# Four graph layers in one pipelined kernel: weight preparations as once-only operations in the engines' lists, and new lists, lags and banks

## The chip, the cores and the metric

One NeuronCore of a Trainium2 chip runs the kernel. The metric is the device time of one execution in microseconds (us). The engines work beside each other, each through its own list of instructions in order, and meet in semaphores: TensorE (PE) multiplies matrices and transposes, and writes to eight banks of PSUM; VectorE (DVE), ScalarE (ACT) and GpSimd (POOL) work elementwise; SyncE (SP) and ACT issue transfers (DMAs).

## The reference

```python
h = relu(layernorm(x)); x = x + L0(h)   # x: (128, 128, 256) f32, adj: (128, 128)
h = relu(layernorm(x)); x = x + L1(h)
h = relu(layernorm(x)); x = x + L2(h)
h = relu(layernorm(x)); x = x + L3(h)
# L0: deg * (h @ Wi.T + b) + adj @ (h @ Wj.T)
# L1: Wh = h @ W; logits e_src[i] + e_dst[j], leaky relu, masked by adj, softmax, attn @ Wh
# L2: the same with 128 columns: concat(alpha @ h', h')
# L3: q, k, v = h @ W.T + b, 8 heads of 32, masked softmax(q k / sqrt(32)) v, then @ Wo.T + bo
```

128 graphs of 128 nodes are independent of each other; all share the adjacency and the weights.

## The kernel before

The 128 graphs are worked off as 64 pairs. A pair has some 100 operations (three to 32 instructions each), and the kernel is a software pipeline over steps t: every engine has one list of operations, `step(t)`, and an operation with lag LAG[name] works in step t on pair t - LAG[name], where there is such a pair (`due`). The order of the entries of LAG (lines 29 to 40) is the order of the calls in the lists: SP's first, then PE's, ACT's, DVE's and POOL's. Steps 7 to 62 are full (PE has lags from -1 to 7); those before are the opening, those after the end. A step's number is a label on each engine: an operation waits for the semaphores of what it needs (`passed`), for the readers of the buffer that it overwrites (`read_before`, buffers of two pairs mostly, one for the exps and probabilities of layer 3), and on PE for the last user of its PSUM bank (`bank_free`, table BANKS in lines 43 to 73: bank, operation that begins the use, operations that free it).

The operations by name, with a number for the layer: `stats`, `mv`, `veps` (DVE) and `rstd`, `y` (POOL) are the layernorm; `h0t` to `h3t` (PE) transpose y; `h.t_hi` (ACT) and `h.t_lo` (DVE) apply relu and split the value into two fp32r parts, since products of that type are made as three matmuls (lines 839 to 841). Layer 0: `m0`, `m1` (PE, the two graphs), `mj_hi` (ACT), `mj_lo` and `t0` (DVE, t0 reads `r0` = x + deg * b of POOL), `s0` (PE, aggregation), `x1` (DVE, line 480). Layer 1: `wh0`, `wh1` by PE as `wh0_mm`, `wh1_mm` and copied by ACT; `dst1` (POOL) gathers the column e_dst; SP writes it to memory (`row_out1`, line 239) and reads it back spread over the partitions (`row_in1`, line 245); `z1` (ACT, line 712) is the leaky relu of the sums, `nmax1` (DVE), `exp1` (ACT), `e1t` (PE), `at1` (ACT), `x2_mm` (PE), `x2` (DVE). Layer 2 is the same with `hh`, `dst2`, `row_out2`, `row_in2`, `z2` and so on, up to `x3` and POOL's `x3_tail`. Layer 3: `qt`, `kt`, `v`, `scores` (PE, 32 matmuls), `nmax3_j` (DVE), `exp3_j` (ACT), `p3_j` (POOL), `pt_j` (PE), `p3t_j` (ACT) for four groups of heads j, `ot` (PE), `ot_hi`, `ot_lo`, `x4_mm` (PE), `x4` (DVE, line 568), `store` (SP). `r3` (POOL) is x3 + bias.

Preparations that happen once stand before the lists or inside one operation's first call: POOL makes deg_b ahead of the first r0 and splits four weights ahead of the first rstd2 (`split_w3`); PE transposes the adjacency before its list, into bank 4, and multiplies weights with the attention vectors ahead of the first s0 (`multiply_weights`), also in bank 4; DVE copies the adjacency and makes the low part of w0 ahead of the first h0t_lo, and splits w1 ahead of the first h1t_lo; ACT rounds w0 ahead of the first h0t_hi.

Of the kernel before, what the change touches and what calls it, by code (L numbers as in the profile page):

```python
# [45 lines left out]
    "h2t": (4, "h2t", ('ht2',)),
    "at2": (3, "e2t", ('at2',)),
    "h1t": (0, "h1t", ('h1t_lo',)),
    "ot": (5, "ot_mm", ('ot_lo',)),
# [1 line left out]
    "sc1": (4, "scores", ('nmax3_1',)),
    "sc2": (3, "scores", ('nmax3_2',)),
    "sc3": (1, "scores", ('nmax3_3',)),
    "hh": (6, "hh_mm", ('hh',)),
    "x3b": (5, "x3_mm", ('x3',)),
    "wh1": (0, "wh1_mm", ('wh1',)),
# [1008 lines left out]
```

## Time and profile before

| | |
|---|---|
| runs | 1285.4, 1282.49, 1284.64 us; median 1284.64 |
| profiled execution | 1286.28 us, span 1284.5 us, clock 0.99 |
| PE busy | 1231.8 us (96%) |
| DVE busy | 1123.6 us (87%) |
| ACT busy | 1049.0 us (82%) |
| POOL busy | 944.6 us (74%) |
| DMA | 55.92 MB, mean 44 GB/s |

Busy time is the time with at least one instruction under way. On PE matmuls overlap, so one that lasts 0.28 us can be followed by the next after 0.12 us: the distance of starts tells the cost, not the duration. The span leaves out what lies around the first and the last instruction. Line numbers are those of the kernel before.

### The profile page before, as it was taken

Reading aid. Unit: us, or ns where it says so; the run is one execution under the profiler, and the core shown is the slowest. Engines: PE = TensorE matmul, PEld = TensorE weight load, DVE = VectorE, ACT = ScalarE, POOL = GpSimd, SP = SyncE. Lnnn points to the kernel's source line nnn. Section 1 sums busy time; section 2 is a strip of 40 time slices with the busy share of each in tenths; the row PEclk is TensorE's granted clock in tenths of the full one; section 3 lists DMA queues with packets and bytes.
Section 4 is the critical chain, followed back from the end, with each engine's and each line's share of the span. In section 5 each row is a group of like instructions: output and inputs, shape, how many; then the busy total and the mean of one; then the engine's idle time right before and its main releaser. Section 6 shows DMA issues by size and latency. Waiting matters only on the chain. (4 is left out here: it accounts for less than half of the span.)

```text
span 1284.5 us, 42963 instructions
## 1 busy us (share of the span) xinstructions
PE 1231.8 (96%) x12177; PEld 1135.2 (88%) x12177; DVE 1123.6 (87%) x5713; ACT 1049.0 (82%) x3907; POOL 944.6 (74%) x1360
## 2 busy tenths in 40 slices
PE   4589999999999999999999999999999999999987
PEld 3478999999999999999999999999999999999886
DVE  3678999999999999999999999999999999998774
ACT  1357888888888888888888888888888888888886
POOL 3657787787778778777777877877787787786654
PEclk8999999999999999999999999999999999999999
DMA  3121212221221221122122122223212212221110
GB/s 117 26 38 30 39 37 45 48 41 40 52 47 35 48 47 37 44 49 44 37 51 48 35 47 47 41 42 51 48 34 48 48 37 46 47 37 29 34 35 34
DMA packets 75768, 55.92 MB, mean 44 GB/s; under 512 B 23568, under 2 KB 75536, under 8 KB 75536
## 3 DMA queue, kind: packets, MB, share of 16 engines
q1 hardware_dynamic: 73472, 51.87, 20.4%
...
q14 instruction: 130, 1.06, 0.5%
...
## 5 line engine op out<-in xcount | busy, mean ns | idle before, releaser
L743 ACT ACTIVATE exps<-masked,nmax 128x128 f32<-128x128 f32 x1024 | 397.5, 400 | 0.0
L306 POOL TENSOR_TENSOR rstd<-veps,power 128x2 f32<-128x2 f32 x256 | 177.9, 695 | 230.3 <-DVE veps L458 230.1
L314 POOL TENSOR_SCALAR y<-x,nm,rstd 128x256 f32<-128x256 f32 x512 | 279.0, 557 | 4.2 <-issue 1.6
L342 POOL TENSOR_TENSOR probs<-exps,rsum 128x512 f32<-128x512 f32 x256 | 263.8, 1041 | 14.2 <-DVE rsum L553 14.2
L545 DVE CUSTOM_DVE_ANT_0 masked<-bank,mask 128x128 f32<-128x128 f32 x1024 | 233.3, 282 | 0.8 <-PE bank L945 0.8
L743 ACT ACTIVATION_READ_ACCUMULATOR exps<-masked,nmax 128x1 f32 x1024 | 203.8, 199 | 0.0
L839 PE MATMUL bank<-w_hi,ht_hi 128*128 128x512 f32 (+1 forms) x512 | 186.5, 364 | 7.0 <-DVE ht_lo L487 7.0
L442 DVE BATCH_NORM_STATS2 stats<-x 128x6 f32<-128x256 f32 x512 | 183.6, 410 | 3.9 <-DMA x<-in_x 3.8
L487 DVE SCALAR_TENSOR_TENSOR ht_lo<-bank,ht_hi 128x512 fp32r<-128x512 f32 x192 | 132.5, 690 | 52.0 <-ACT ht_hi L681 50.0
L849 PE MATMUL bank<-ident,y 128*128 128x128 f32 x1024 | 155.4, 275 | 21.6 <-POOL y L314 20.1
L841 PE MATMUL bank<-w_hi,ht_lo 128*128 128x512 f32 (+1 forms) x512 | 175.5, 343 | 0.0
L840 PE MATMUL bank<-w_lo,ht_hi 128*128 128x512 f32 (+1 forms) x512 | 175.3, 342 | 0.0
L681 ACT ACTIVATE ht_hi<-bank 128x512 fp32r<-128x512 f32 x192 | 114.8, 598 | 60.6 <-PE bank L849 60.4
L953 PE MATMUL bank<-ident,probs 128*128 128x128 f32 x1024 | 154.0, 274 | 3.7 <-POOL probs L342 1.8
L751 ACT ACTIVATE probs3t<-bank 128x512 f32<-128x512 f32 x256 | 152.2, 596 | 2.6 <-PE bank L953 2.6
L849 PEld LDWEIGHTS bank<-ident,y 128*128 128x128 f32 x1024 | 121.7, 142 | 33.1 <-POOL y L314 23.1
L953 PEld LDWEIGHTS bank<-ident,probs 128*128 128x128 f32 x1024 | 121.9, 141 | 11.8 <-POOL probs L342 3.9
L839 PEld LDWEIGHTS bank<-w_hi,ht_hi 128*128 128x128 f32 x512 | 98.4, 192 | 15.1 <-DVE ht_lo L487 8.5
L699 ACT ACTIVATE ht<-bank 128x512 f32<-128x512 f32 x64 | 38.2, 597 | 89.2 <-PE bank L849 89.2
L841 PEld LDWEIGHTS bank<-w_hi,ht_lo 128*128 128x128 f32 x512 | 98.1, 192 | 12.0
L840 PEld LDWEIGHTS bank<-w_lo,ht_hi 128*128 128x128 f32 x512 | 98.7, 193 | 6.4
L721 ACT ACTIVATE ez<-z,nmax 128x128 f32<-128x128 f32 x256 | 100.2, 393 | 2.1 <-DVE nmax L497 1.6
...
## 6 DMA issues: line engine op xcount, KB each, us to landing
x<-in_x SPq DMA_DIRECT2D x64, 256.0 KB, 5.5
db<-rows SPq DMA_DIRECT2D x128, 128.0 KB, 3.7
out<-x SPq DMA_DIRECT2D x64, 256.0 KB, 6.2
rows<-dst SPq DMA_DIRECT2D x128, 1.0 KB, 4.1
...
w_sb<-in_w ACTq DMA_DIRECT2D x1, 256.0 KB, 4.0
probs<-in_w1t ACTq DMA_DIRECT2D x1, 256.0 KB, 4.4
exps<-in_wot SPq DMA_DIRECT2D x1, 256.0 KB, 7.9
```

The source lines that it names most:

```text
L306: pool.tensor_tensor(rstd[i][:, b], veps[i][:, b], power[:], ALU.pow).then_inc(S[f"rstd{i}"], 1)
L314: last = pool.tensor_scalar(y[i][:, b, g], src[:, bx, g], nm[i][:, s, g:g + 1], rstd[i][:, s, g:g + 1], ALU.add, ALU.mult)
L342: pool.tensor_tensor(probs3[:, p % BUFFERS["probs3"], j], exps3[:, p % BUFFERS["exps3"], j], rsum3[:, s, j].unsqueeze(2).to_broadcast([P, ...
L442: last = dve.bn_stats(stats[i][:, b, g], src[:, bx, g])
L545: last = dve.tensor_tensor_reduce(masked3[:, b, j, i], bank_of(f"sc{j}")[:, i * P:(i + 1) * P], mask[:], scale=-1.0, scalar=-MASKED, op0=A ...
L743: last = act.activation(exps3[:, b, j, i], masked3[:, p % BUFFERS["masked3"], j, i], ACT.Exp, bias=nmax3[:, s, j, i:i + 1], scale=-1.0, ac ...
L751: act.activation(probs3t[:, b, j].rearrange("p b n -> p (b n)"), bank_of(f"pt{j}")[:], ACT.Copy).then_inc(S[f"p3t_{j}"], 1)
L839: pe.matmul(out_ap, lhs[0], rhs[0], start=start, stop=False)
L840: pe.matmul(out_ap, lhs[0], rhs[1], start=False, stop=False)
L841: return pe.matmul(out_ap, lhs[1], rhs[0], start=False, stop=stop)
L849: last = pe.transpose(bank_of(f"h{i}t")[:, (c * G + g) * P:(c * G + g + 1) * P], y[i][:, b, g, c * P:(c + 1) * P], ident[:])
L953: last = pe.transpose(bank_of(f"pt{j}")[:, i * P:(i + 1) * P], probs3[:, p % BUFFERS["probs3"], j, i], ident[:])
```

## The change

All lags, lists and banks are new; the once-only work becomes operations of its own in the lists, each with a lag that is its only step (`t == LAG[name]`), a semaphore, and for PE's two an entry in BANKS (`prepa`, `prep`). The rounding of the four layer-3 weights moves from POOL to ACT (`w3_high`), the four subtractions stay on POOL as `w3_low0` to `w3_low3` (wk, wq, wv, wo). The users wait for the new semaphores. The transfer of the bias moves from SP's fourth place to ACT's first, and ACT's loads of w1 and w2 behind its first activation. The loads' lag goes from -5 to -3. PE's lags are the old ones. The logits' rows go by transfers in both kernels.

```diff
 LAG = {
+       "row_out2": 3, "row_out1": 1, "row_in2": 3, "row_in1": 1, "store": 7, "load": -3, "qt_mm": 5, "h2t": 3, "kt_mm": 5, "h1t": 1, "e2t": 4,
+       "hh_mm": 3, "ot_mm": 7, "scores": 5, "adj_spread": -1, "x3_mm": 4, "wh1_mm": 1, "wh0_mm": 1, "e1t": 2, "pt3": 6, "h0t": -1, "x2_mm": 2,
+       "v_mm": 5, "s0": 0, "pt0": 6, "pt2": 6, "products": 0, "pt1": 6, "h3t": 4, "x4_mm": 7, "m1": -1, "m0": -1, "exp3_2": 5, "v": 5, "p3t_0": 6,
+       "p3t_2": 6, "w3_high": 0, "h3t_hi": 4, "z2": 3, "p3t_1": 6, "exp3_3": 5, "mj_hi1": -1, "mj_hi0": -1, "exp2": 3, "ht2": 2, "exp3_0": 5,
+       "h1t_hi": 0, "at2": 3, "w0_high": -3, "z1": 1, "hh": 2, "ot_hi": 6, "exp3_1": 5, "exp1": 1, "wh1": 0, "wh0": 0, "at1": 1, "p3t_3": 5,
+       "h0t_hi": -2, "nmax3_2": 5, "x3": 4, "rsum1_any": 2, "rsum3_1": 6, "stats3": 4, "rsum1": 2, "mv3": 4, "veps3": 4, "nmax3_3": 5, "h0t_lo": -1,
+       "x2": 2, "stats2": 2, "rsum3_2": 5, "mv2": 2, "adj_rows": -1, "nmax3_0": 5, "veps2": 2, "x1": 0, "h3t_lo": 4, "mv0": -2, "stats1": 0, "mv1": 0,
+       "veps0": -2, "veps1": 0, "nmax2": 3, "w1_split": 0, "x4": 7, "t0_1": -1, "nmax3_1": 5, "mj_lo1": -1, "mj_lo0": -1, "rsum3_3": 5, "t0_0": -1,
+       "qt": 4, "w0_low": -2, "kt": 4, "rsum3_0": 5, "rsum2": 3, "h1t_lo": 0, "nmax1": 1, "stats0": -3, "ot_lo": 6, "r0": -1, "rstd2": 2, "y2": 2,
+       "rstd1": 0, "y1": 0, "r3": 5, "w3_low2": 3, "x3_tail": 3, "p3_3": 5, "w3_low1": 1, "deg_b_made": -3, "rstd0": -2, "dst2": 2, "y0": -2,
+       "p3_0": 5, "dst1": 0, "p3_1": 5, "rstd3": 3, "y3": 3, "p3_2": 4, "w3_low0": 0, "w3_low3": 1,
 }
 BANKS = {
+    "qt": (0, "qt_mm", ('qt',)),
+    "h2t": (1, "h2t", ('ht2',)),
     "kt": (2, "kt_mm", ('kt',)),
+    "h1t": (3, "h1t", ('h1t_lo',)),
+    "at2": (4, "e2t", ('at2',)),
+    "hh": (5, "hh_mm", ('hh',)),
+    "ot": (1, "ot_mm", ('ot_lo',)),
     "sc0": (2, "scores", ('nmax3_0',)),
+    "sc1": (6, "scores", ('nmax3_1',)),
+    "sc2": (0, "scores", ('nmax3_2',)),
+    "sc3": (4, "scores", ('nmax3_3',)),
+    "prepa": (0, "adj_spread", ('adj_rows',)),
+    "x3b": (3, "x3_mm", ('x3',)),
+    "wh1": (5, "wh1_mm", ('wh1',)),
+    "wh0": (1, "wh0_mm", ('wh0',)),
+    "at1": (0, "e1t", ('at1',)),
+    "pt3": (5, "pt3", ('p3t_3',)),
+    "h0t": (3, "h0t", ('h0t_lo',)),
+    "x2b": (1, "x2_mm", ('x2',)),
+    "v": (5, "v_mm", ('v',)),
+    "x1b": (0, "s0", ('x1',)),
     "pt0": (3, "pt0", ('p3t_0',)),
+    "pt2": (4, "pt2", ('p3t_2',)),
+    "prep": (2, "products", ('w1_split',)),
+    "pt1": (5, "pt1", ('p3t_1',)),
+    "h3t": (1, "h3t", ('h3t_lo',)),
+    "x4b": (3, "x4_mm", ('x4',)),
+    "m1": (4, "m1", ('mj_lo1', 't0_1')),
+    "m0": (5, "m0", ('mj_lo0', 't0_0')),
 ...
@@ SP
-            sp.dma_start(deg_b[:], bias0.partition_broadcast(P)).then_inc(b0_in, 16)
@@ POOL
-                pool.wait_ge(deg_b_made, 1)
-            def split_w3():
-                pool.wait_ge(wk_in, 32)
 ...
-                for w, (hi, lo) in ((wk_sb, wk_r), (wq_sb, wq_r), (wv_sb, wv_r), (wo_sb, wo_r)):
-                    pool.tensor_copy(hi[:], w).then_inc(w3_high, 1)
 ...
+            def low_w3(i):
+                w, (hi, lo) = ((wk_sb, wk_r), (wq_sb, wq_r), (wv_sb, wv_r), (wo_sb, wo_r))[i]
+                pool.wait_ge(S["w3_high"], i + 1)
+                pool.tensor_tensor(lo[:], w, hi[:].bitcast(F32), ALU.subtract).then_inc(S[f"w3_low{i}"], 1)
             def biased_x0(p):
                 pool.wait_ge(x_in[bx], (p // BUFFERS["x0"] + 1) * 16)
+                pool.wait_ge(S["deg_b_made"], 1)
@@ DVE: the low part of w0 leaves prepare_rows
+            def low_w0():
+                dve.wait_ge(S["w0_high"], 1)
+                dve.tensor_tensor(w0_r[1][:], w0_sb, w0_r[0][:].bitcast(F32), ALU.subtract).then_inc(S["w0_low"], 1)
@@ ACT
-            act.dma_start(w1_sb[:, :, 0:D], w1.rearrange("(c p) o -> p c o", p=P)).then_inc(w1_in, 16)
+            act.dma_start(deg_b[:], bias0.partition_broadcast(P)).then_inc(b0_in, 16)
 ...
             act.activation(warm[:], power[:], ACT.Exp)
+            act.dma_start(w1_sb[:, :, 0:D], w1.rearrange("(c p) o -> p c o", p=P)).then_inc(w1_in, 16)
+            act.dma_start(w2_sb[:, :, 0:F1], w2.rearrange("(c p) o -> p c o", p=P)).then_inc(w2_in, 16)
 ...
+            def round_w3():
+                act.wait_ge(wk_in, 32)
 ...
+                for w, (hi, lo) in ((wk_sb, wk_r), (wq_sb, wq_r), (wv_sb, wv_r), (wo_sb, wo_r)):
+                    act.activation(hi[:], w, ACT.Copy).then_inc(S["w3_high"], 1)
@@ PE
+            def spread_adjacency():
+                pe.wait_ge(adjacency, 1)
+                bank_free(pe, "prepa", 0)
+                pe.transpose(bank_of("prepa")[:, 0:P], adj_f[:], ident[:]).then_inc(S["adj_spread"], 1)
             def multiply_weights():
-                pe.wait_ge(adj_t, 1)
+                bank_free(pe, "prep", 0)
 ...
@@ PE, project_transposed and project_v
-                pe.wait_ge(w3_split, 4)
+                for i in range(4):
+                    pe.wait_ge(S[f"w3_low{i}"], 1)
```

## Rows read from the trace of the kernel before

**Rows 1.** The table of stretches: us, busy us and (count) per engine, PEclk, DMA share, GB/s.
```profile
0.00:28.20 28.20, 11.65 (x40) 9.15 (x41) 8.78 (x32) 4.50 (x7) 9.68 (x17) 0.93 0.44 133
28.20:137.60 109.40, 88.59 (x633) 76.35 (x633) 83.37 (x383) 60.56 (x208) 71.59 (x110) 0.92 0.18 30
137.60:1192.20 1054.60, 1054.60 (x10636) 980.38 (x10635) 970.61 (x4974) 911.57 (x3415) 813.76 (x1171) 1.00 0.22 43
1192.20:1284.50 92.30, 76.93 (x875) 69.28 (x873) 60.85 (x326) 72.35 (x279) 49.55 (x62) 0.98 0.16 36
```

**Rows 2.** The source view of line 480, 200 to 1180 us.
```profile
L480 DVE TENSOR_TENSOR x<-bank,t x52: 690/690/693, 212.9 to 1174.0; 128x512 f32<-128x512 f32 x52
```

**Rows 3.** Timeline of the opening: start us, us, engine, line, operation, [idle before <-releaser].
```profile
5.85 0.74 DVE L442 BATCH_NORM_STATS2 stats<-x 128x6 f32<-128x256 f32 x2
...
9.17 0.61 POOL L289 TENSOR_TENSOR deg_b<-deg_b,deg 128x256 f32<-128x256 f32 x1 [7.68 <-DMA deg_b<-in_b]
...
10.90 0.75 DVE L442 BATCH_NORM_STATS2 stats<-x 128x6 f32<-128x256 f32 x2 [3.76 <-DMA x<-in_x]
...
11.98 2.14 POOL L314 TENSOR_SCALAR y<-x,nm,rstd 128x256 f32<-128x256 f32 x2 [0.19 <-POOL rstd L306]
...
14.17 1.12 PE L849 MATMUL bank<-ident,y 128*128 128x128 f32 x4 [8.43 <-POOL y L314]
...
25.26 2.06 PE L834 MATMUL bank<-exps,bv_sb 128*128 128x256 f32 x4
...
28.21 0.69 DVE L480 TENSOR_TENSOR x<-bank,t 128x512 f32<-128x512 f32 x1 [3.19 <-PE bank L867]
```

**Rows 4.** Timeline of POOL, 48 to 62 us.
```profile
49.61 0.61 POOL L298 CAST wk_hi<-exps 128x512 fp32r<-128x512 f32 x1
...
55.55 1.26 POOL L301 TENSOR_TENSOR wo_lo<-exps,wo_hi 128x512 fp32r<-128x512 f32 x1
```

**Rows 5.** Timeline of SP's queue, 63 to 92 us.
```profile
63.89 0.32 SPq L239 DMA_DIRECT2D rows<-dst  x1
...
68.66 0.32 SPq L245 DMA_DIRECT2D db<-rows  x1
...
69.08 0.59 SPq L239 DMA_DIRECT2D rows<-dst  x1
```

**Rows 6.** Timeline of ACT near the end.
```profile
1218.84 0.67 ACT L712 ACTIVATE bank<-db,wh 128x128 f32<-128x128 f32 x2 [2.49 <-DMA db<-rows]
```

**Rows 7.** Timeline of PE in one full step.
```profile
429.61 1.08 PE L965 MATMUL bank<-probs3t,v 128*32 128x128 f32 x32
...
431.72 1.16 PE L886 MATMUL bank<-w_sb,ht 128*128 128x130 f32 x8
...
432.72 0.61 PE L910 MATMUL bank<-hh,at 128*128 128x128 f32 x4
...
434.60 0.38 PE L902 MATMUL bank<-ident,ez 128*128 128x128 f32 x2
...
434.82 0.60 PE L953 MATMUL bank<-ident,probs 128*128 128x128 f32 x4
```

**Rows 8.** Timeline of ACT in the same step.
```profile
430.90 0.60 ACT L757 ACTIVATE ot_hi<-bank 128x512 fp32r<-128x512 f32 x1
...
431.38 0.41 ACT L743 ACTIVATE exps<-masked,nmax 128x128 f32<-128x128 f32 x1
...
432.92 0.39 ACT L705 ACTIVATE hh<-bank 128x260 f32<-128x260 f32 x1
...
434.80 0.39 ACT L693 ACTIVATE wh<-bank 128x258 f32<-128x258 f32 x1 [0.33 <-PE bank L841]
```

**Rows 9.** DMA issues, KB each, us to landing: 12 to 40 us, then 300 to 1100 us.
```profile
x<-in_x SPq DMA_DIRECT2D x3, 256.0 KB, 2.6
...
x<-in_x SPq DMA_DIRECT2D x43, 256.0 KB, 5.6
out<-x SPq DMA_DIRECT2D x43, 256.0 KB, 6.3
```

More of the change, by code:

```diff
@@ L29 @@
 LAG = {
[10 rows of a table removed]
[11 rows of a table added]
 }
 BANKS = {
-    "qt": (6, "qt_mm", ('qt',)),
+    "qt": (0, "qt_mm", ('qt',)),
+    "h2t": (1, "h2t", ('ht2',)),
     "kt": (2, "kt_mm", ('kt',)),
[L46 to L49, printed above, removed]
+    "h1t": (3, "h1t", ('h1t_lo',)),
+    "at2": (4, "e2t", ('at2',)),
+    "hh": (5, "hh_mm", ('hh',)),
+    "ot": (1, "ot_mm", ('ot_lo',)),
     "sc0": (2, "scores", ('nmax3_0',)),
[L51 to L56, printed above, removed]
-    "wh0": (3, "wh0_mm", ('wh0',)),
-    "at1": (6, "e1t", ('at1',)),
-    "pt3": (0, "pt3", ('p3t_3',)),
-    "h0t": (5, "h0t", ('h0t_lo',)),
-    "pt0": (3, "pt0", ('p3t_0',)),
-    "x2b": (6, "x2_mm", ('x2',)),
-    "pt2": (0, "pt2", ('p3t_2',)),
-    "x1b": (1, "s0", ('x1',)),
-    "v": (3, "v_mm", ('v',)),
-    "m0": (2, "m0", ('mj_lo0', 't0_0')),
-    "h3t": (0, "h3t", ('h3t_lo',)),
-    "pt1": (6, "pt1", ('p3t_1',)),
-    "m1": (5, "m1", ('mj_lo1', 't0_1')),
-    "x4b": (1, "x4_mm", ('x4',)),
+    "sc1": (6, "scores", ('nmax3_1',)),
[11 more added lines that the diff above has]
+    "x1b": (0, "s0", ('x1',)),
+    "pt0": (3, "pt0", ('p3t_0',)),
+    "pt2": (4, "pt2", ('p3t_2',)),
[5 more added lines that the diff above has]
+    "m0": (5, "m0", ('mj_lo0', 't0_0')),
     "zz2": (7, "z2", ('nmax2',)),
@@ L171, in gnn_kernel @@
         bank = [ctx.enter_context(nc.psum_tensor(f"bank{i}", [P, 512], F32)) for i in range(8)]
-        preparation = bank[4]
         def bank_of(task):
@@ L180, in gnn_kernel @@
         w0_in, w1_in, w2_in, wk_in, wq_in, wv_in, wo_in = [sem(f"{name}_in") for name in ("w0", "w1", "w2", "wk", "wq", "wv", "wo")]
[L181 to L183 removed]
+        constants, adjacency, w1_whole, w1_high, c3_made = [sem(name) for name in ("constants", "adjacency", "w1_whole", "w1_high", "c3_made")]
         x_in = [sem(f"x_in{i}") for i in range(BUFFERS["x0"])]
         x_out = [sem(f"x_out{i}") for i in range(BUFFERS["x4"])]
[L188 removed]
+        S = {name: sem(name) for name in LAG if name not in ("row_out2", "row_out1", "row_in2", "row_in1", "store", "load")}
         for name in ("nm0", "nm1", "nm2", "nm3",):
@@ L214, in bank_free @@
                 q = step - LAG[begun_by]
-                if other == number and 0 <= q < NP:
+                if other == number and 0 <= q < (1 if TASKS[i] in ("prepa", "prep") else NP):
                     for name in freed_by:
@@ L351, in step @@
             def step(t):
+                if due(t, "r0"):
+                    biased_x0(t - LAG["r0"])
+                if due(t, "rstd2"):
+                    inverse_deviation(2, t - LAG["rstd2"])
+                if due(t, "y2"):
+                    normalise(2, x2, t - LAG["y2"])
+                if due(t, "rstd1"):
+                    inverse_deviation(1, t - LAG["rstd1"])
+                if due(t, "y1"):
+                    normalise(1, x1, t - LAG["y1"])
+                if due(t, "r3"):
+                    biased_x3(t - LAG["r3"])
+                if t == LAG["w3_low2"]:
+                    low_w3(2)
+                if due(t, "x3_tail"):
+                    x3_tail(t - LAG["x3_tail"])
+                if due(t, "p3_3"):
+                    normalise_p3(3, t - LAG["p3_3"])
+                if t == LAG["w3_low1"]:
+                    low_w3(1)
+                if t == LAG["deg_b_made"]:
+                    prepare_deg_b()
+                if due(t, "rstd0"):
+                    inverse_deviation(0, t - LAG["rstd0"])
+                if due(t, "dst2"):
+                    gather_dst(2, hh, "hh", "hh", F1 + 1, t - LAG["dst2"])
+                if due(t, "y0"):
+                    normalise(0, x0, t - LAG["y0"])
+                if due(t, "p3_0"):
+                    normalise_p3(0, t - LAG["p3_0"])
+                if due(t, "dst1"):
+                    gather_dst(1, wh, "wh", last_of("wh0", "wh1"), D + 1, t - LAG["dst1"])
                 if due(t, "p3_1"):
@@ L926, in project_v @@
                 passed(pe, "h3t_lo", p)
-                pe.wait_ge(w3_split, 4)
+                for i in range(4):
+                    pe.wait_ge(S[f"w3_low{i}"], 1)
                 bank_free(pe, "v", p)
```

284 lines of the change are left out of this document (127 added, 157 removed), and 10 rows, old and new, of the table LAG.

## The prediction

> **What bounds the kernel now.** I read the table of stretches first [rows 1]. Columns: length, busy time and count of each engine, granted clock, DMA share, GB/s. Between 137.6 and 1192.2 us TensorE (PE) is busy in all of 1054.60 us at clock 1.00; VectorE (DVE) has 970.61 (92%), ScalarE (ACT) 86%, GpSimd (POOL) 77%. In the stretch there are 52 starts of the sum after layer 1 (x1, L480) from 212.9 to 1174.0 [rows 2]: 961.1 / 51 = 18.84 us per pair. The reader should see that 64 x 18.84 = 1206 us is PE's own work and that 1284.5 - 1206 = 78.5 us is all that an order of work alone can give back: PE idles 16.6 + 20.8 us in the opening (stretches 1 and 2 of rows 1) and 15.4 us at the end; the rest is half-clock time (0.93, 0.92, 0.98) and pipe filling. A list that makes PE wait in every step, though, costs 56 times (steps 7 to 62 are full).
>
> The change alters no PE operation and no PE lag: the PE pipeline stays 8 steps deep, and 18.84 us is the floor per full step. So the sum has an opening, an end, and a possible slip per full step.
>
> **A. Until the first x1 (28.21 us before).** POOL sat idle 7.68 us until the bias row had landed, made deg_b at 9.17, then r0, then rstd, and y0 only at 11.98, which took 2.14; the first transposes are at 14.17, on an engine idle for 8.43 us; the last four of the ten products of weights run at 25.26 for 2.06 us, ahead of the aggregation, and x1 starts at 28.21 [rows 3]. Now the bias is the first transfer of the ACT queue, r0 stands behind y0, and the products behind the aggregation. Statistics start at 5.85 for 0.74, some 0.5 more for mean and shift: 7.1; rstd 0.7: 7.9; y0 2.14: 10.0; transposes 1.12 and the ACT copy 0.6: 11.8. DVE holds the second tile's statistics before that (10.90 to 11.65, waiting for its landing), so it is free. ht_lo 0.7: 12.5 instead of 16.65. From there x1 took 11.56 us; 3.3 of it were the ten products and their weights (the timeline has them from 23.4 to 26.7, those of 25.26 last), so x1 starts at 12.5 + 8.3 = 20.8. Taken: -7.5. Ends: -4 (only the y0 part) and -10 (products and clock both kind). The products, 3.3 us or less, now delay m1 and m0 of pair 1, beside which x1, its statistics, rstd and y1 (some 3.5 us) and the split of w1 (2 us) run anyway: nothing, at worst +3, inside the ends.
>
> **B. Splitting the layer-3 weights.** Eight POOL operations from 49.61 to 56.81, 0.61 and 1.26 each, stood ahead of rstd and y [rows 4]: 7.2 us on the path, PE idle for 6 us behind them. Now ACT rounds them (4 x 0.6 = 2.4 us, step 0, where ACT next waits for m1; it has 48.8 of 109.4 us free in stretch 2 of rows 1) and POOL's four subtractions of 1.26 lie singly in steps 0, 1, 1 and 3, POOL being free for 38 of 109 us there. Each stands just after dst1 or y1, with at least 2 us until the next statistics. Taken: -6. Ends -3 (half come back) and -7.2.
>
> **C. Order of the row transfers, and y1 apart from y2.** SP issued layer 2's row at 63.89, and only after its landing the spread at 68.66 and layer 1's row at 69.08 [rows 5], though dst1 was ready at 66.3: 2.8 us, in the next step 2.3. The new SP list issues both rows before either spread. DVE and POOL now finish stats2, rstd2, y2 ahead of x1, stats1, y1, so y1 no longer queues behind y2: about 1 us per step in steps 2 to 4. PE work (15 us and more) bounds steps 5 and 6. Taken: -3. Ends 0 and -5.
>
> **D. The end.** In step 65 ACT idles 2.49 us before layer 1's logits, for a spread whose row was issued behind a store [rows 6]; PE then waits 2.0 and 1.1 us. The new list has the store after the spreads. The last chain (four exps of 1.54 us, POOL's probs, transposes, attention, projection) is the same. Taken: -3.5, ends 0 and -6.
>
> **E. A slip per full step.** In the new banks table pt3 takes bank 5, last used by wh1, so pt3 waits for ACT's copy of wh1. PE time from ot's start to pt3's: ot and scores 2.11 (429.61 to 431.72), x3 and the two wh 1.88 (432.72 to 434.60), e1t 0.22: 4.21; the 1.00 of hh now lies before ot [rows 7]. ACT's list in that time: ot_hi, exp3_1, exp1, wh1, for hh is now ahead of ot_hi. ot takes 1.08, ot_hi to the next 0.48, four exps 1.54, two more 0.77, the copy 0.39 [rows 7, 8], a semaphore 0.05: 4.31. ACT is not behind before ot_hi (ht2, exp3_0, h1t_hi, at2, z1, hh end 0.4 us before ot does). The loop ot - ACT - wh1 - pt3 - rest of the list - ot is therefore 0.10 too long, and a matmul that follows a wait is followed 0.05 later than in a stream: +0.15 per step, 56 steps, +8.4. Ends: 0 (ACT a tenth faster than its rows) and 0.3 (x2, which needs at1 1.1 us after e1t with 0.25 to spare, slips too), +17.
>
> A rule of the Trainium skill bears on that price: TensorE: Matmul & The Clock Gate (specifications table) says that the queue reorders in part and pulls weight loads ahead of matmuls in flight. If the waiting transposes' loads went ahead the slip would be nearer 0.05 per step, +3; the stalled matmuls of this trace show load and matmul starting together (both at 14.17), so I do not use it.
>
> The other reuses that I followed through the new lists have over 0.3 us: x4b after pt0 in bank 3 0.4, at1 to x2 0.25, wh0 after ot 0.8, e1t after sc2 0.7, h0t after x3b 0.9.
>
> **Sum** against the profiled run: 1286.28 us around a span of 1284.5. -7.5 - 6 - 3 - 3.5 + 8.4 = -11.6: 1274.7. The median of the runs shown, 1284.64, is 1.6 under the profiled run, so 1273.0.
>
> **Rivals.**
> 1. No slip. Speaks for it: a tenth of a us is within what overlapping ACT operations hide. Against: both sums come from rows of full steps. 1273.0 - 8.4 = 1264.6.
> 2. The load lands too late (slower). Lag -5 becomes -3, the lag of the statistics that read it, and the load is queued behind the store, which waits for x4. Loop in DVE: x4 - store issued 0.45 - load issued and landed L - stats0 - ot_lo - nmax3_2 - ... - x4. DVE is busy 17.3 us per step (970.61 / 1054.60 x 18.84); the operations outside this loop (t0, nmax3_1, mj_lo, qt, kt, h1t_lo, nmax1 and the small ones) make 5.2 of it, and small ones waiting for the one before add about 1: 13.1. The period is 13.5 + L, so it binds from L = 5.3. Loads landed in 2.6 us alone, in 5.6 in full steps, when they follow a row transfer and others come behind, stores in 6.3 [rows 9]. Ends for L: 2.6 and 6.3 or more. I take 4: the rows have landed by then, only the store is ahead. With L = 6.1 it is +0.8 x 56 = +45 and in place of E: 1273.0 - 8.4 + 45 = 1310. It decides from L = 5.3 + 20 / 56 = 5.7: above, the kernel is slower than before. The DMA chapter of the Trainium skill (DMA: Bandwidth & Descriptors, Queues, rings and completion order) speaks for this one: a completion increment is a strongly ordered write that lands only after all earlier writes of its DMA engine, so a load cannot report before the store has been written. By that rule L is at least the store's own landing less the 0.5 us between the issues, 5.8 if stores stay as they are in full steps; the trace has no load behind a store, so it neither shows nor excludes it.
> 3. The opening gains are given back: PE's half clock falls elsewhere, and products and subtractions delay steps 1 to 3. Half of A to C lost, 8.3: 1281.3. For it: three of the four half-clock spells lie where PE had waited; against: each edit takes away a wait seen in the trace.
> 4. The change does not do what it says: the opening steps are bound by the row transfers (rows, spread, logits, max, exps, e1t: 9.4 us from dst1) so that only the wait of B goes and E stays: 1286.3 - 6 + 8.4 - 1.6 = 1287, near the old time.
>
> **Chances.** Forecast 0.46 (1262 to 1281 for itself), no slip 0.22, late load 0.16, opening given back 0.12, row transfers 0.04. A measurement of this kernel can tell about 0.2%, 2.6 us, from no change. Faster by more: 0.45 + 0.22 + 0.02 + 0.07 = 0.76 (from the first four cases in this order); within: 0.01 + 0.01 + 0.03 + 0.02 = 0.07; slower: 0.13 + 0.02 + 0.02 = 0.17 (late load, opening, row transfers). The range takes in the first two whole and the third: 1262 to 1286.
>
> **What would show it.** x1 (L480's successor) first at about 20.8 us and for the eighth time at about 121 (A to C); no eight POOL operations in a row, deg_b near 5.5 us; SP issuing two rows back to back; no 2.49 us of ACT before the last logits. E: PE waits of about 0.1 us per full step for ACT's wh before transposes of probs, period 18.95 to 19.05. Rival 1: period 18.84. Rival 2: DVE stats waiting for DMA x in every full step, period above 19.2. I am wrong altogether if another engine pair waits more than 0.4 us in each full step, or if x1 comes first later than 24 us.

## The result

The changed kernel takes 1278.85 us (median of 8 runs, 1275.96 to 1279.74), the kernel before 1284.0 beside it (8 runs, 1282.49 to 1286.38): ratio 0.9959, 95% interval 0.9947 to 0.997. The forecast was 1273.0. The direction held and the time lies in the range, but the gain is 5.2 us where 11.6 were forecast.

The profiled execution took 1278.44 us around a span of 1276.6. Its table of stretches, cut at the same three events as [rows 1] (first x1, eighth x1, last x1, end), has the same columns: length, busy us and count for PE, PEld, DVE, ACT and POOL, granted clock, DMA share, GB/s.

```profile
0.00:22.44 22.44, 8.35 (x33) 6.33 (x33) 8.47 (x31) 5.87 (x10) 8.44 (x16) 1.00 0.60 167
22.44:123.89 101.45, 88.81 (x656) 77.14 (x656) 84.02 (x390) 61.91 (x211) 69.94 (x107) 0.95 0.20 32
123.89:1189.68 1065.79, 1065.79 (x10639) 986.88 (x10638) 1024.53 (x4977) 925.05 (x3416) 817.16 (x1173) 1.00 0.21 43
1189.68:1276.60 86.92, 75.19 (x858) 67.69 (x856) 60.03 (x321) 71.54 (x277) 48.76 (x61) 0.98 0.15 33
```

| stretch | before | after | change | forecast |
|---|---|---|---|---|
| to the first x1 (A) | 28.2 | 22.4 | -5.8 | -7.5 |
| to the eighth x1 (B, C) | 109.4 | 101.5 | -7.9 | -9.0 |
| 56 full steps (E) | 1054.6 | 1065.8 | +11.2 | +8.4 |
| from the last x1 (D) | 92.3 | 86.9 | -5.4 | -3.5 |
| span | 1284.5 | 1276.6 | -7.9 | -11.6 |

The kernel won 19.1 us outside the full steps and gave 11.2 back in them. Length less PE's busy time, from the two tables, tells where: between the first and the eighth x1 PE idles 12.6 us instead of 20.8 and is busy as long as before (88.8 us), so B and C are waits taken away. Up to the first x1 it idles 14.1 instead of 16.6 and is busy for 8.35 us instead of 11.65: most of the products now stand behind x1, and the granted clock is 1.00 instead of 0.93 (kernel 6).

**The opening**, as a timeline (start, us, engine, line, operation, idle before and its releaser), against [rows 3]:

```profile
7.31 0.23 DVE L395 CAST adj_f<-adj_i 128x128 f32<-128x128 int32 x1 [7.31 <-DMA adj_i<-in_adj]
...
8.24 0.74 DVE L441 BATCH_NORM_STATS2 stats<-x 128x6 f32<-128x256 f32 x2
...
10.45 2.13 POOL L304 TENSOR_SCALAR y<-x,nm,rstd 128x256 f32<-128x256 f32 x2 [0.19 <-POOL rstd L296]
...
22.44 0.68 DVE L479 TENSOR_TENSOR x<-bank,t 128x512 f32<-128x512 f32 x1
```

y0 comes at 10.45, earlier than the 11.98 of before but not at the 7.9 of the forecast: DVE starts its statistics at 8.24 instead of 5.85, for it idles until adj lands (deg_b, foreseen near 5.5, comes at 8.02). The bias, now first on ACT's queue, is the reason (kernel 5 below).

**Weights and rows.** The four subtractions of POOL lie singly; the first and the last of them, against [rows 4], then SP's queue, which now issues two rows together and then two spreads, against [rows 5]:

```profile
32.53 1.28 POOL L291 TENSOR_TENSOR wk_lo<-exps,wk_hi 128x512 fp32r<-128x512 f32 x1
...
63.57 1.27 POOL L291 TENSOR_TENSOR wv_lo<-exps,wv_hi 128x512 fp32r<-128x512 f32 x1
```

```profile
53.77 2.56 SPq L237 DMA_DIRECT2D rows<-dst  x2
57.81 1.20 SPq L243 DMA_DIRECT2D db<-rows  x2
```

**A full step.** The source view of the x1 sum (200 to 1180 us) gives (1171.1 - 200.3) / 51 = 19.035 us per pair, against 18.84 in [rows 2]. The timeline of PE and that of ACT show where, against [rows 7, 8]:

```profile
L479 DVE TENSOR_TENSOR x<-bank,t x52: 676/678/692, 200.3 to 1171.1; 128x512 f32<-128x512 f32 x52
```

```profile
460.17 0.43 PE L919 MATMUL bank<-ident,ez 128*128 128x128 f32 x2
460.53 0.63 PE L972 MATMUL bank<-ident,probs 128*128 128x128 f32 x4
460.99 0.60 PE L864 MATMUL bank<-ident,y 128*128 128x128 f32 x4
```

```profile
459.63 0.39 ACT L731 ACTIVATE ez<-z,nmax 128x128 f32<-128x128 f32 x1
459.92 0.19 ACT L731 ACTIVATION_READ_ACCUMULATOR ez<-z,nmax 128x1 f32 x1
460.01 0.74 ACT L703 ACTIVATE wh<-bank 128x258 f32<-128x258 f32 x2
```

From e1t's start to pt3's it is 0.36 us where it was 0.22, and pt3 to h0t takes 0.46 instead of 0.44. Two things of ACT end just there: exp1 at 460.11, which e1t reads, and the copy of wh1, the first of the two L703 copies, at about 460.4, which bank 5 waits for. The weight loads show that pt3's transposes are held up as a whole: before, the load of the first starts 0.11 us ahead of its matmul (434.71 and 434.82), now only 0.03 (460.50 and 460.53):

```profile
434.71 0.47 PEld L953 LDWEIGHTS bank<-ident,probs 128*128 128x128 f32 x4
```

```profile
460.50 0.31 PEld L972 LDWEIGHTS bank<-ident,probs 128*128 128x128 f32 x3
```

PE is "busy" for every one of the 1065.79 us all the same: matmuls overlap, so a stall of 0.1 us leaves no idle time and no row in the view of waits. The sign that I had named, a wait of 0.1 us per step, could not appear; only the distance between starts shows it, and that lies where the other sign had it, 18.95 to 19.05.

**Transfers**, 300 to 1100 us (KB each, median us from issue to landing), against [rows 9]; and layer 1's last logits, against the 2.49 us of idle time in [rows 6]:

```profile
x<-in_x SPq DMA_DIRECT2D x43, 256.0 KB, 2.9
...
out<-x SPq DMA_DIRECT2D x42, 256.0 KB, 2.2
```

```profile
1211.70 0.70 ACT L722 ACTIVATE bank<-db,wh 128x128 f32<-128x128 f32 x2
```

### The profile page after: what moved, and what is told of

It is laid out like the page before. It is cut to its first block, busy times and chain, and to the rows that moved or that the text cites. A ratio compares the mean times of both kernels' runs of the same rounds, so it can differ in the third digit from the quotient of the medians.

```text
span 1276.6 us, 43416 instructions
## 1 busy us (share of the span) xinstructions
PE 1238.1 (97%) x12177; PEld 1138.0 (89%) x12177; DVE 1177.1 (92%) x5713; ACT 1064.4 (83%) x3911; POOL 944.3 (74%) x1356
## 4 chain that ended last, share of the span: by engine, by line
PE 90%; ACT 2%; DVE 2%; issue 1%; DMA 0%; POOL 0%; ACTq 0%; SPq 0%; DVEq 0%; POOLq 0%
PE bank L854 16%; PE bank L856 16%; PE bank L855 16%; PE bank L972 9%; PE bank L864 8%; PE bank L927 7%; PE bank L964 5%; PE bank L984 5%; PE bank L903 4%; PE bank L919 2%; PE bank L883 2%; ACT exps L753 1%; DMA db<-rows 0%; DVE stats L441 0%; ACT probs3t L761 0%
## 5 line engine op out<-in xcount | busy, mean ns | idle before, releaser
L753 ACT ACTIVATION_READ_ACCUMULATOR exps<-masked,nmax 128x1 f32 x1024 | 197.5, 193 | 0.0
L441 DVE BATCH_NORM_STATS2 stats<-x 128x6 f32<-128x256 f32 x512 | 190.0, 412 | 2.7 <-issue 0.3
L854 PE MATMUL bank<-w_hi,ht_hi 128*128 128x512 f32 (+1 forms) x512 | 181.0, 354 | 6.2 <-DVE ht_lo L486 5.1
L761 ACT ACTIVATE probs3t<-bank 128x512 f32<-128x512 f32 x256 | 145.6, 595 | 28.5 <-PE bank L972 28.4
L972 PE MATMUL bank<-ident,probs 128*128 128x128 f32 x1024 | 136.0, 276 | 2.6 <-POOL probs L333 2.5
L972 PEld LDWEIGHTS bank<-ident,probs 128*128 128x128 f32 x1024 | 115.0, 142 | 19.8 <-POOL probs L333 3.0
L854 PEld LDWEIGHTS bank<-w_hi,ht_hi 128*128 128x128 f32 x512 | 97.5, 190 | 17.9 <-DVE ht_lo L486 6.8
L856 PEld LDWEIGHTS bank<-w_hi,ht_lo 128*128 128x128 f32 x512 | 97.5, 190 | 11.9
L697 ACT ACTIVATE mj_hi<-bank 128x256 fp32r<-128x256 f32 x128 | 47.8, 376 | 55.6 <-PE bank L856 55.5
```

The lines of the kernel that those rows point to most:

```text
L441: last = dve.bn_stats(stats[i][:, b, g], src[:, bx, g])
L753: last = act.activation(exps3[:, b, j, i], masked3[:, p % BUFFERS["masked3"], j, i], ACT.Exp, bias=nmax3[:, s, j, i:i + 1], scale=-1.0, ac ...
L761: act.activation(probs3t[:, b, j].rearrange("p b n -> p (b n)"), bank_of(f"pt{j}")[:], ACT.Copy).then_inc(S[f"p3t_{j}"], 1)
L854: pe.matmul(out_ap, lhs[0], rhs[0], start=start, stop=False)
L856: return pe.matmul(out_ap, lhs[1], rhs[0], start=False, stop=stop)
L972: last = pe.transpose(bank_of(f"pt{j}")[:, i * P:(i + 1) * P], probs3[:, p % BUFFERS["probs3"], j, i], ident[:])
```

## The experiments

The kernels of one group ran on one chip with the kernel before beside them, 4 to 12 runs of each. Every kernel has one profile of its own. Eight profiles of kernels that start as the changed kernel does have their first x1 between 22.4 and 23.0 us, and two profiles of the changed kernel itself have the eighth at 123.9 and 125.6: in the opening a difference under 2 us between single profiles says nothing. Most of it is TensorE's clock: the second step takes 11.9 us at a granted clock of 1.00 in the first profile of the changed kernel and 13.3 at 0.87 in the other (kernel 0), at the same idle time of PE (2.5 and 2.4 us). So where the opening is compared below, PE's idle time between the first and the eighth x1 stands beside it; it is 12.3 to 12.6 us in the four profiles whose lists are the changed kernel's there or nearly so (its own, kernels 0, 2 and 8).

### Group 1: the slip and the weights (kernel before 1284.48 us)

**Kernel 1, banks 3 and 5 exchanged from pt3 on.**

```diff
-    "pt3": (5, ...), "h0t": (3, ...), "v": (5, ...), "pt0": (3, ...), "pt1": (5, ...), "x4b": (3, ...), "m0": (5, ...)
+    "pt3": (3, ...), "h0t": (5, ...), "v": (3, ...), "pt0": (5, ...), "pt1": (3, ...), "x4b": (5, ...), "m0": (3, ...)
```

> The changed kernel with the two banks 3 and 5 exchanged from the transposes of probs 3 to the end of a step (pt3 3, h0t 5, v 3, pt0 5, pt1 3, x4b 5, m0 3), so that pt3 follows x3b, not wh1, and no longer waits for ACT's copy of wh1. The changed kernel's full step is 19.03 us against 18.845, with e1t's start to pt3's 0.355 instead of 0.217. Theory W (the slip is waiting on ACT, in two parts): pt3's wait for the copy of wh1 makes 0.11 of it and goes; e1t ties with exp1 (0.05) and stays: period 18.92, 57 x 0.11 = 6.4 us less than the changed kernel, ratio to before 0.991. Theory of the prediction (the whole slip is the bank): 18.87, 9 us less, 0.989. Rival L (the slip is PE's own list: more changes between kinds of matmul): 19.03, no gain, 0.996.

Measured: 1277.9 us, 0.9955 [0.9939, 0.9971]. The median step is 18.92, as theory W said. Its timeline of PE:

```profile
460.58 0.43 PE L919 MATMUL bank<-ident,ez 128*128 128x128 f32 x2
460.85 0.60 PE L972 MATMUL bank<-ident,probs 128*128 128x128 f32 x4
```

0.27 from e1t to pt3: the bank's 0.09 is gone (and 0.03 behind pt3), 0.05 stays. But the time missed the expected 0.991: PE idled 14.4 us between the first and the eighth x1 instead of 12.6, the end took 88.4 us instead of 86.9, and the full steps won 4.0 us in all where 56 times 0.115 would be 6.4, one step near 582 us taking 19.7. The exchange creates waits elsewhere (kernel 3).

**Kernel 2, exp1 ahead of exp3_1.**

```diff
+                if due(t, "exp1"):
+                    exps(1, "rsum1_any", t - LAG["exp1"])
                 if due(t, "exp3_1"):
                     exps3_of(1, t - LAG["exp3_1"])
-                if due(t, "exp1"):
-                    exps(1, "rsum1_any", t - LAG["exp1"])
```

> The changed kernel, with ACT's exp1 ahead of exp3_1 (both behind ot_hi); the banks as in the changed kernel. exp1 ends 1.54 us earlier, the copy of wh1 not at all. Theory W: e1t's loads are on time, but pt3 still waits for the copy of wh1, which stands where it stood: period 19.03, ratio to before 0.996. If the tie of exp1 with e1t were the whole cause: 18.87 and 0.989. Rival L: 19.03. A danger named beforehand: exp3_1 ends 0.77 us later; if probs 1 is late with it, pt1 waits and the period grows over 19.03.

Measured: 1277.77 us, 0.9951 [0.9936, 0.9966]; the step is 19.03 and e1t to pt3 0.36, as expected of W. e1t is now on time, but pt3 waits for the copy of wh1 where it stood. The tie alone is not the cause.

**Kernel 3, both.**

> The changed kernel with both edits: banks 3 and 5 exchanged and exp1 ahead of exp3_1. Theory W: both waits are gone, period 18.86, 57 x 0.17 = 9.7 us less than the changed kernel, ratio to before 0.9885, about 1269 us. Theory of the prediction: no more than the banks alone. Rival L: 19.03, ratio 0.996.

Measured: 1273.53 us, 0.9925 [0.9905, 0.9945]; the median step is 18.874, e1t to pt3 0.22 as before the change:

```profile
458.52 0.38 PE L919 MATMUL bank<-ident,ez 128*128 128x128 f32 x2
458.74 0.60 PE L972 MATMUL bank<-ident,probs 128*128 128x128 f32 x4
```

So the slip had two waits that shared one place: 19.035 - 18.92 = 0.115 for the bank, 18.92 - 18.874 = 0.05 for exp1 once the bank's is gone (alone, in kernel 2, nothing), and 0.03 is left over 18.845 for the rest of the list. The total missed W's 0.9885, for the exchange costs elsewhere: PE idles 14.5 us between the first and the eighth x1 instead of 12.6 (the eighth x1, at 124.9, does not show it, for the granted clock is 0.97 there instead of 0.93 to 0.95), and the end takes 88.9 us instead of 86.9. PE's waits in the opening (first row), then in the end (second):

```profile
PE bank L864 <- DVE t L471: 5.0, 4, 1.6
```

```profile
PE bank L972 <- DVE x L527: 2.2, 2, 1.2
```

In short steps h1t now waits for DVE's reading of m0, and pt3 for DVE's reading of x3b; neither wait exists in the changed kernel.

**Kernel 4, the layer-3 weights split on POOL again** (eight operations ahead of layer 2's first rstd, ACT's four roundings gone).

```diff
                 if due(t, "rstd2"):
+                    if t == LAG["rstd2"]:
+                        split_w3()
                     inverse_deviation(2, t - LAG["rstd2"])
```

> The changed kernel with step B undone: POOL again makes the rounding and the subtraction of the four layer-3 weights, eight operations in a row ahead of layer 2's first rstd. Theory (B as predicted, by what it measured): 7.5 us of POOL stand again ahead of rstd2, rstd1, y1; x1 for the eighth time 4 to 6 us later than 123.9, the full steps at 19.03 as they are, so +4 to +6 us: ratio to before 0.999 to 1.001. Rival (what B gave came from the new order of DVE and POOL, layer 2 ahead of layer 1, and not from the weights): under +2 us, 0.996 to 0.9975.

Measured: 1285.64 us, 1.0008 [0.9998, 1.0018]; the eighth x1 at 131.8, 6.2 to 7.9 us later, step 3 takes 17.9 us as it did before the change, the full step is the same. PE's waits for y, 6.3 us in the changed kernel:

```profile
PE bank L866 <- POOL y L314: 9.9, 5, 5.3
```

PE idles 16.0 us between the first and the eighth x1 instead of 12.6, and it is busy 92.8 us instead of 88.8 to 90.1, at a granted clock of 0.89 (0.62 in step 3). So the eight operations on POOL's path are shown to cost time in the new lists, some 3.4 us of it as waits and the rest by PE's clock behind them; that they cost 6 in the old ones, as I took, is not measured.

### Group 2: opening and transfers (kernel before 1290.5 us)

On this chip the kernel before was 6 us slower than elsewhere, so these ratios are compared with one another and not with 0.996. The changed kernel did not run there; kernel 6, whose eighth x1, full step and end are those of its profiles, is the nearest to it.

**Kernel 5, the bias late.**

```diff
-            act.dma_start(deg_b[:], bias0.partition_broadcast(P)).then_inc(b0_in, 16)
             act.dma_start(w1t_sb, ...)
...
             act.dma_start(a2_sb[:], a2).then_inc(w2_in, 16)
+            act.dma_start(deg_b[:], bias0.partition_broadcast(P)).then_inc(b0_in, 16)
...
+                if t == LAG["deg_b_made"]:
+                    prepare_deg_b()
                 if due(t, "r0"):
```

> The changed kernel with the broadcast of the bias fifth on ACT's queue, not first, and POOL's deg_b moved in its list to just ahead of r0(0), behind y0(0). Theory (step A fell short because the broadcast, 128 KB read from one row of 1 KB, runs beside x(0), adj and w0t and slows them: in the changed kernel they landed at 7.06, 7.29 and 9.89 us, before at 4.35, 4.90 and 7.28): they land again near 4.4, 4.9 and 7.3, the statistics start near 5.8, the first x1 comes at 19.9 to 20.8 instead of 22.4, and about 2 us of it last to the end: ratio to before 0.994 to 0.995. Rival (the landings are slow for another reason, such as the order of the queue's issues): x(0) still at 7 us, first x1 at 22.4, ratio 0.996.

Measured: 1275.12 us, 0.9878 [0.9854, 0.9903]. The timeline of DVE has adj and the statistics back at the times of before, and the first x1 at 20.63, within 0.2 us of the forecast's 20.8; the eighth at 120.0:

```profile
4.92 0.23 DVE L395 CAST adj_f<-adj_i 128x128 f32<-128x128 int32 x1 [4.92 <-DMA adj_i<-in_adj]
...
5.84 0.74 DVE L441 BATCH_NORM_STATS2 stats<-x 128x6 f32<-128x256 f32 x2
...
20.63 0.68 DVE L479 TENSOR_TENSOR x<-bank,t 128x512 f32<-128x512 f32 x1
```

The terms on the way hold too: y0 at 8.06 (forecast 7.9), ht_lo done at 12.65 (12.5). That x1 lands within 0.2 is luck in part, for kernel 9, with the same opening, has its first x1 at 19.11. And of the 3.9 to 5.6 us by which the eighth x1 is earlier only 1.8 to 2.3 come from the first: step 1 took 10.1 us here at a granted clock of 1.00, and 11.2 to 11.6 at 0.85 in both profiles of the changed kernel. Kernel 9 has the bias late and 0.85 in that step, so this does not come of the bias.

The stretch from 2 to 5 us of the changed kernel, then of this one (the last two columns are DMA share and GB/s):

```profile
2.00:5.00 3.00, 0.00 (x0) 0.00 (x0) 0.00 (x0) 1.04 (x1) 0.00 (x0) 1.00 0.81 145
```

```profile
2.00:5.00 3.00, 0.00 (x0) 0.00 (x0) 0.08 (x1) 1.49 (x2) 0.00 (x0) 1.00 0.91 278
```

The DMA engines are occupied in both, but with the broadcast at the head they move half as much. Kernel 5 is 5.5 us faster than kernel 6 beside it, without overlap of their runs; the products differ as well.

**Kernel 6, the ten products ahead of the aggregation.**

```diff
+                if t == LAG["products"]:
+                    multiply_weights()
                 if due(t, "s0"):
                     aggregate(t - LAG["s0"])
```

> The changed kernel with PE's ten products of weights ahead of the aggregation of pair 0, as before the change. Theory (part of A): the products, 2.0 us here, stand again on the path to the first x1: 24.4 instead of 22.4; of it 1 to 2 us last until x1 for the eighth time (123.9), ratio to before 0.9965 to 0.9975. Rival (whatever stands behind the aggregation, the split of w1 is what the next projection waits for): x1 first 2 us later, but the second at 34.0 as it was, ratio 0.996.

Measured: 1280.63 us, 0.9918 [0.9898, 0.9938]. The first x1 came at 23.0, the eighth at 124.0. The products take 2 us as expected; PE had been waiting 0.49 us for DVE's mj_lo in their place, and the aggregation starts 1.2 us later than in the changed kernel (22.16 instead of 20.93):

```profile
20.14 0.51 PE L845 MATMUL bank<-a_sb,probs 128*128 128x2 f32 x4
...
22.16 0.58 PE L883 MATMUL bank<-mj_hi,aggr_r 128*128 128x512 f32 x1
```

In the changed kernel the first x1 was not waiting for the aggregation at all, which had ended by 21.7: it stood behind DVE's own ht_lo (21.85, 0.67 us). So 2 us on PE cost 0.6, inside the spread, and nothing of it lasts to the eighth x1.

That does not make the products worthless in the kernel before. There x1 idled 3.19 us for the aggregation behind them [rows 3], and its ht_lo was done by 25.0. The same work, ten products and the aggregation, took PE 4.7 us there and 2.9 here. The two stretches, before and in this kernel, have the granted clock behind the busy times, 0.58 and 1.00:

```profile
23.50:28.20 4.70, 4.70 (x21) 4.15 (x20) 0.69 (x1) 0.60 (x1) 0.83 (x1) 0.58 0.00 0
```

```profile
20.14:23.02 2.88, 2.88 (x21) 2.68 (x20) 2.07 (x5) 2.83 (x6) 0.00 (x0) 1.00 0.32 91
```

So 1.8 us of what the first x1 won is TensorE's clock, 0.58 in that stretch before and 1.00 in the new lists, with or without the products in their old place. PE had idled 1.42 us just ahead of that stretch; what keeps the clock up in the new lists was not tried.

**Kernel 7, layer 2's spread ahead of layer 1's row.**

```diff
                 if due(t, "row_out2"): ...
-                if due(t, "row_out1"): ...
                 if due(t, "row_in2"): ...
+                if due(t, "row_out1"): ...
```

> The changed kernel with layer 2's spread ahead of layer 1's row in SP's list (row_out2, row_in2, row_out1, row_in1), as before the change; the store stays behind them. Theory (step C): layer 1's row waits for layer 2's row to land, 2.6 to 3 us, in steps where both are there: steps 5 and 6 of the opening 1 to 4 us longer, the end 1 to 2 us longer, the full step 19.03 as before: ratio to before 0.998 to 1.000. Rival (what C gave came from the normalisation of layer 2 ahead of layer 1): under 1 us, 0.996 to 0.9965.

Measured: 1284.99 us, 0.9958 [0.9941, 0.9974]; the eighth x1 at 131.2, 5.6 to 7.3 us later, more than expected; step 7 alone takes 22.7 us instead of 18.4 to 18.7, with a wait of PE for ACT's copies of probs, which stand behind layer 2's logits in ACT's list:

```profile
PE bank L854 <- ACT probs3t L761: 3.5, 1, 3.5
```

Those logits wait for a slow spread, not for a late row as expected. The spread is issued at 104.10, layer 1's row right behind it at 104.52; no store is under way, and yet the spread lands after 7.7 us and the row after 7.4:

```profile
111.78 0.67 ACT L722 ACTIVATE bank<-db,hh 128x128 f32<-128x128 f32 x2 [3.10 <-DMA db<-rows]
```

```profile
rows<-dst SPq DMA_DIRECT2D x1, 1.0 KB, 7.4
```

The end is 86.9, as it was: SP's order between the layers is worth nothing there. In all it is 4.4 us slower than kernel 6.

**Kernel 8, the store ahead of layer 1's spread.**

```diff
                 if due(t, "row_in2"): ...
+                if due(t, "store"): ...
                 if due(t, "row_in1"): ...
-                if due(t, "store"): ...
```

> The changed kernel with the store ahead of layer 1's spread in SP's list (row_out2, row_out1, row_in2, store, row_in1). Theory (step D: the end gained because layer 1's spread no longer waits behind a store, for x4): from x4 for the first time on, layer 1's spread is issued only behind x4, 7 us later than now in a full step, and in the end ACT again stands 2 to 4 us idle ahead of layer 1's last logits: the end from the last x1 on (86.9 us) 2.5 to 4 us longer. In full steps the spread would be issued at 451.5 and land near 455.8, just where ACT's logits start (455.96): 0 to 0.3 us per step, up to +17: ratio to before 0.998 to 1.012. Rival (D's gain is from the rest of the list): the end as long as now, and 0.996.

Measured: 1283.61 us, 0.9944 [0.9924, 0.9964]. The full steps took 4.5 us more in all, through waits of ACT for layer 1's spread (total us, times, longest):

```profile
ACT bank L722 <- DMA db<-rows: 8.5, 17, 1.2
```

The end took 87.3 instead of 86.9: as a theory of D this one fell. A store that holds only the spread back costs the end under 0.5 us; in time the kernel is 3.0 us slower than kernel 6, by its full steps.

### Group 3: what is left open, and the best version (kernel before 1283.61 us)

**Kernel 0, the changed kernel again.**

> The changed kernel as it is, on the chip of the three kernels beside it, to compare with: x1 first near 22.5 us, for the eighth time near 124, full step 19.03, end (from the last x1) 87.0, ratio to before 0.996.

Measured: 1277.8 us, 0.9964 [0.995, 0.9978]; x1 at 22.9 and 125.6, step 19.04, end 86.6.

**Kernel 10, the kernel before with its store behind layer 1's row and spread.**

```diff
-                if due(t, "store"): ...
                 if due(t, "row_out1"): ...
                 if due(t, "row_in1"): ...
+                if due(t, "store"): ...
```

> The kernel before the change with one edit: SP's store stands behind layer 1's row and spread (row_out1, row_in1, store, row_out2, load, row_in2), not ahead of them. Theory (step D, and what the store costs: in the end of the kernel before, a store issued 0.37 us behind a spread took 7.5 us to land, and layer 1's row issued 0.52 us behind it 7.2, against 3.0 to 3.2 alone): the row no longer has the store ahead of it and lands in 3 to 4 us, ACT's idle 2.49 us ahead of the last logits is gone, the end 2 to 3.5 us shorter than 92.3, step 7 of the opening (20.5 us, a first store in it or not) perhaps shorter too, the full step 18.85: ratio to before 0.9975 to 0.9985. Rival (the spread in flight, not the store, slows the row): the row still takes 6 to 7 us, the end 92.3, ratio 1.000.

Measured: 1279.51 us, 0.9972 [0.9962, 0.9982]. The transfers issued between 1207.9 and 1216 us in the kernel before (KB, us to landing), then the matching ones here, 1201.9 to 1213:

```profile
out<-x SPq DMA_DIRECT2D x1, 256.0 KB, 7.6
...
rows<-dst SPq DMA_DIRECT2D x1, 1.0 KB, 7.2
```

```profile
out<-x SPq DMA_DIRECT2D x1, 256.0 KB, 4.6
...
rows<-dst SPq DMA_DIRECT2D x1, 1.0 KB, 4.6
```

This row of 1 KB took 7.2 us with a spread and a store in flight, 4.6 with the spread alone. One pair of rows overstates it, for kernel 7's row took 7.4 without a store. Over the whole profiles, a row issued with a spread and a load under way took 4.8 us in the median here (58 rows, 3.6 to 6.8), and with a store as well 5.8 in the kernel before (48 rows, 3.5 to 7.1): the store adds about 1 us, and the rest of the spread from row to row is not explained. ACT's idle time ahead of the last logits fell from 2.49 to 0.40 us:

```profile
1210.95 0.68 ACT L712 ACTIVATE bank<-db,wh 128x128 f32<-128x128 f32 x2 [0.40 <-DMA db<-rows]
```

and the end from 92.3 to 89.9. So the edit takes D's wait away in this pair of profiles: it is the store ahead of the row, not of the spread. This one line moved makes 3.6 us, by the ratio, in a kernel whose full step stays at 18.84. (Its eighth x1 came at 132.5 instead of 137.6; 2.1 us of that lie ahead of the first x1, at 26.12 instead of 28.21, where nothing was edited. So the one profile of the kernel before lies high in its opening, and up to 2 of the 5.8 us that A won against it may be chance.)

**Kernel 11, DVE's and POOL's old order of the two layers in the first steps.**

```diff
                 if due(t, "x2"): ...
+                if t < 7 and due(t, "x1"): ...
                 if due(t, "stats2"): ...
+                if t < 7 and due(t, "stats1"): ...
...
                 if due(t, "rstd2"): ...
+                if t < 7 and due(t, "rstd1"): ...
                 if due(t, "y2"): ...
```

> The changed kernel with DVE's and POOL's order of the two layers in steps up to 6 as before the change: x2, x1, stats2, stats1, mv2, mv1, and the shifts likewise, POOL's rstd1 ahead of y2; SP's list as in the changed kernel. Theory (the other half of step C): y1 queues again behind layer 2's normalisation, about 1 us in each of steps 2 to 4: x1 for the eighth time 2 to 3 us later than in the changed kernel, the rest the same: ratio to before 0.998. Rival (all of C was SP's order, which by itself made 7.3 us in the changed lists): 0 to 0.5 us, 0.996.

Measured: 1284.88 us, 1.0014 [1.0003, 1.0026]; the eighth x1 at 130.7, 5.1 us after kernel 0's and 6.8 after that of the changed kernel's first profile, where 2 to 3 were expected. PE's waits between 25 and 135 us, here and then in the changed kernel:

```profile
PE bank L874 <- POOL y L304: 7.2, 5, 2.8
PE bank L864 <- DVE ht_lo L488: 5.8, 4, 2.0
```

```profile
PE bank L864 <- POOL y L304: 6.3, 6, 1.5
PE bank L854 <- DVE ht_lo L486: 3.7, 3, 1.4
```

The waits are what theory C says, 3.0 us more of these two, 2.3 more idle time in all (15.0 us). The larger part is not a wait: PE is busy for 93.8 us between the first and the eighth x1 instead of 88.8 to 90.1, at a granted clock of 0.91 (0.68 in step 3).

**Kernel 9, the combination.** exp1 ahead of exp3_1, the bias late, and the banks exchanged only where steps are long:

```diff
+        def number_of(task, step):
+            number = BANKS[task][0]
+            if task in SWAPPED and 8 <= step < NP:
+                return 8 - number
+            return number
```

> The changed kernel with what the runs before this one point to: exp1 ahead of exp3_1, the bias late with deg_b behind y0(0), and banks 3 and 5 exchanged only in steps 8 to 63. Where they were exchanged in all steps (with exp1 ahead), h1t waited for DVE's t0 in the opening, 5.0 us, and pt3 for DVE's x3 in the end, 2.2 us. Theory W with these side costs: x1 for the eighth time at 120 to 121, full step 18.87, end 87: span about 1265, ratio to before 0.985 to 0.987, 11 us less than the changed kernel. Rival (the side costs are not the exchange of banks but ACT's order): end 88.9 and eighth x1 at 122, 1269.

Measured: 1266.01 us (4 runs, 1264.74 to 1267.19), 0.987 [0.9856, 0.9884], against 1277.8 of the changed kernel beside it. Its table of stretches:

```profile
0.00:19.11 19.11, 8.63 (x33) 6.54 (x33) 8.65 (x31) 5.88 (x10) 8.27 (x16) 1.00 0.63 196
19.11:120.95 101.84, 89.27 (x656) 77.27 (x656) 83.98 (x390) 62.01 (x211) 70.32 (x107) 0.95 0.21 32
120.95:1178.71 1057.76, 1057.13 (x10639) 987.59 (x10638) 1011.66 (x4978) 925.55 (x3416) 820.47 (x1173) 1.00 0.21 44
1178.71:1264.20 85.49, 73.72 (x858) 66.09 (x856) 59.88 (x321) 71.37 (x277) 48.88 (x61) 1.00 0.14 34
```

Opening, full step and span are where theory W put them, the end is 1.5 us better than its 87. PE idles 12.6 us between the first and the eighth x1 and 11.8 in the end, as in the changed kernel (12.6 and 11.7), where kernel 3 had 14.5 and 13.9: the side costs belonged to the exchange of banks in short steps. The 1.5 us at the end are PE's clock again, 1.00 over the stretch instead of 0.98. This version beats both kernels.

## Why the prediction was right in kind and wrong in size

The forecast was 5.85 us too low. Its terms, in the order of their share:

- **E, 2.8 us: the mis-sized step.** "+0.15 per step, 56 steps, +8.4" measured +0.19 to +0.20, +11.2. The mechanism was right: kernels 1 and 3 take the wait for the copy of wh1 away. It was 0.115 per step, less than the 0.15 taken. What failed is that the rest of the slip was put at nothing: I followed the reuses of banks and did not ask the same of e1t's own input. Moving hh ahead of ot took 1.00 us of PE's work out from between ot and e1t. By the prediction's own rows exp1 then ends 3.87 + 0.05 us after ot's start and e1t begins at 3.99, with 0.07 to spare; it was late, and cost 0.05 per step. The last 0.03 is the new list's own and is not explained further. The Trainium skill (TensorE: Matmul & The Clock Gate, specifications table) has weight loads pulled ahead of matmuls in flight, by which the wait would have been nearer 0.05. The trace does not agree for this stalled transpose: its load started 0.03 us ahead of its matmul, against 0.11 in a stream.
- **The step from profile to median, 2.1 us.** I took 1.6 off for the runs' median. The profiled execution of before lay 2.3 over the median of its eight runs, that of the changed kernel 0.4 under its own. No run gives this a mechanism: it is the spread of single runs.
- **A, 1.7 us.** y0 ahead of deg_b and r0 worked, but "statistics start at 5.85" did not hold: the broadcast put first on ACT's queue slowed x(0), adj and w0t. Kernel 5 moves it, and x1 comes at 20.63 as forecast. I had counted what waits for the bias, and not what waits behind it. The "3.3 us" of the products were read rightly as the way of before (x1 idled 3.19 for what stood behind them) but wrongly as their work: it is 2.0 us at the clock of the new lists, kernel 6 shows that they cost at most 0.6 of the first x1 there, and 1.8 us of the gain are the granted clock, 1.00 instead of 0.58.
- **B and C, 1.1 us.** Forecast -6 and -3, together -7.9. Undone one at a time in the changed kernel, the weights cost 6.2 to 7.9, SP's order 5.6 to 7.3, the order of the layers 5.1 to 6.8: some 17 to 22 for three parts that together won 7.9. The parts are not additive. Part of the excess is PE's clock: the three kernels idle 16.0, 16.7 and 15.0 us between the first and the eighth x1 against 12.6, so 2.3 to 4.1 us of each cost are waits, and PE is busy 1.5 to 5.0 us longer for the same work, at 0.89 to 0.92 instead of 0.93 to 0.95. The waits, put together, make 9.8 us, near the 8.2 by which PE's idle time fell from before. What each part won on its own from before is not measured.
- **D, -1.9 us.** -5.4 instead of -3.5, within its ends. Kernel 10 shows 2.4 of it for the store; the rest, with hh's copy no longer behind the exps, is read from the traces and not tried alone.

**The rivals.** No slip (0.22): excluded, the step is 19.035. The late load (0.16): excluded; it rested on a landing of 5.6 to 6.3 us, and in the new order the load lands in 2.9 and the store in 2.2, below the 5.3 at which it would bind. The rule beside it, that a completion increment lands only after the earlier writes of its DMA engine (the Trainium skill, DMA: Bandwidth & Descriptors, Queues, rings and completion order), agrees with the row of 1 KB of the kernel before, which landed just after the store ahead of it (7.6 us for the store, 7.2 for the row issued 0.5 later), and with kernel 7's behind its spread. It gives no durations: the store itself fell from 6.3 to 2.2, so what it bounded was small. Opening given back: a sixth of A to C (13.7 instead of 16.5), most of it for the bias. PE's half clock, which that rival named, did not grow elsewhere: the granted clock is 1.00 to the first x1 and 0.95 up to the eighth, against 0.93 and 0.92. The change not doing what it says: no.
